# Two loads of the first block's rows move from SyncE's queue to ScalarE's

## The reference

```
scale = cond @ norm_w.T + 1.0
ms = mean(x * x, axis=-1)
h = x * (scale[:, None, :] * rsqrt(ms + EPS))
val, gate = split(h @ up_w.T)
h = val * gelu(gate)
y = act_quant(h) @ weight_quant(down_w).T + x
```

## Time and profile before

| | before |
|---|---|
| median of 3 runs | 745.76 us (745.72 to 745.92) |
| the profiled execution, its whole time | 745.96 us |
| its span, from the first to the last instruction | 744.1 us |
| TensorE busy | 734.2 us (99%) |
| VectorE busy | 564.0 us (76%) |
| ScalarE busy | 347.6 us (47%) |
| mean granted TensorE clock | 0.999 |

### The profile page before, as it was taken

How to read it: one execution, slowest core, us unless ns; L and a number is a source line. 1 busy time by engine, 2 the same in 40 slices (tenths; PEclk the granted TensorE clock), 3 DMA queues, 4 the chain that set the end, 5 groups by cost and what they waited for, 6 DMA issues and landing times.

```text
span 744.1 us, 14385 instructions
## 1 busy us (share of the span) xinstructions
PE 734.2 (99%) x5510; PEld 538.2 (72%) x5510; DVE 564.0 (76%) x1126; ACT 347.6 (47%) x677; POOL 101.7 (14%) x137
## 2 busy tenths in 40 slices
PE   7999999999999999999999999999999999999998
PEld 6544444444678887888778887788878887788864
DVE  5567778999888776888669875888758876586657
ACT  5889766433364442364334542355324443244424
POOL 1211477877230000000000000000000000000000
PEclk9999999999999999999999999999999999999999
DMA  8877583848554453443634445343543334363202
GB/s 326 304 264 237 183 281 118 282 164 250 181 172 130 143 188 117 122 145 104 201 108 142 128 131 161 114 160 100 155 150 103 101 100 130 118 179 104 96 30 85
DMA packets 44277, 117.35 MB, mean 158 GB/s; under 512 B 5424, under 2 KB 5680, under 8 KB 43056
## 3 DMA queue, kind: packets, MB, share of 16 engines
q1 hardware_dynamic: 44208, 116.42, 48.3%
HBM read 99.62 MB, written 16.78 MB: 156 GB/s over the span
## 4 chain that ended last, share of the span: by engine, by line
PE 96%; DVE 2%; DMA 1%; issue 1%; ACT 0%; SPq 0%; POOL 0%; DVEq 0%; ACTq 0%; POOLq 0%
PE ps_v L585 14%; PE ps_v L586 14%; PE ps_v L587 14%; PE ps_y L713 13%; PE ps_g L585 6%; PE ps_g L587 6%; PE ps_g L586 6%; PE ps_v L603 4%; PE ps_g L605 4%; PE ps_v L605 4%; PE ps_v L604 4%; PE ps_g L604 4%; PE ps_g L603 4%; PE ps_v L792 1%; DMA q<-in_up_t_dram 1%
## 5 line engine op out<-in xcount | busy, mean ns | idle before, releaser
L585 PE MATMUL ps_v<-x_hi,w_hi 128*128 128x256 f16 x968 | 263.9, 273 | 1.5 <-DVE ps_v L1155 0.8
L587 PE MATMUL ps_v<-x_hi,w_lo 128*128 128x256 f16 x968 | 263.9, 273 | 0.0
L586 PE MATMUL ps_v<-x_lo,w_hi 128*128 128x256 f16 x968 | 263.8, 273 | 0.0
L817 ACT COPY ps_g<-ps_v 128x256 f32<-128x256 f32 x96 | 34.3, 357 | 205.8 <-PE ps_v L587 205.8
L828 ACT ACTIVATE g<-ps_g,w_unscale 128x512 f32<-128x512 f32 x128 | 87.3, 682 | 69.6 <-PE ps_g L587 69.6
L1155 DVE TENSOR_TENSOR ps_v<-ps_v,p 128x256 f32<-128x256 f32 x96 | 41.3, 430 | 95.3 <-PE ps_v L587 95.0
L835 ACT ACTIVATE g<-h 128x512 f32<-128x512 f32 x128 | 81.3, 635 | 63.3 <-DVE h L1167 63.0
L585 PE MATMUL ps_g<-x_hi,w_hi 128*128 128x256 f16 x392 | 106.8, 273 | 0.1
L586 PE MATMUL ps_g<-x_lo,w_hi 128*128 128x256 f16 x392 | 106.8, 273 | 0.0
L587 PE MATMUL ps_g<-x_hi,w_lo 128*128 128x256 f16 x392 | 106.8, 273 | 0.0
L585 PEld LDWEIGHTS ps_v<-x_hi,w_hi 128*128 128x128 f16 x968 | 94.7, 98 | 15.8 <-DVE ps_v L1155 1.0
(11 more groups left out here) (139 smaller groups left out, 936.3 us busy)
## 6 DMA issues: line engine op xcount, KB each, us to landing
w_lo<-w_lo_dram SPq DMA_DIRECT2D x96, 448.0 KB, 3.3
q<-in_up_t_dram SPq DMA_DIRECT2D x16, 512.0 KB, 4.8
xt<-in_x_cols_dram SPq DMA_DIRECT2D x8, 1024.0 KB, 4.9
res<-in_x_rows_dram SPq DMA_DIRECT2D x26, 256.0 KB, 3.6
out_dram<-res SPq DMA_DIRECT2D x26, 256.0 KB, 2.8
xs<-in_x_rows_dram SPq DMA_DIRECT2D x22, 256.0 KB, 3.7
w_lo_dram<-w_lo SPq DMA_DIRECT2D x16, 256.0 KB, 4.4
dw<-in_down_t_dram SPq DMA_DIRECT2D x8, 512.0 KB, 6.4
```

Source lines behind the costliest of these rows:

```text
L585: pe.matmul(to, w_hi[:, wh:wh + P], hi, start=start and kt == 0, stop=False, skip_group_check=True)
L586: pe.matmul(to, w_hi[:, wh:wh + P], lo, start=False, stop=False, skip_group_check=True)
L587: last = pe.matmul(to, w_lo[:, wl:wl + P], hi, start=False, stop=(kt == 1), skip_group_check=True)
```

## The change

The two loads of `xs_first` leave SyncE's program and stand at the top of ScalarE's program, ahead of its first activation. Their sizes, sources, destinations and semaphores stay, and nothing waits before them. SyncE's program issues the first piece of weights directly behind `norm_sb`.

```
@@ SyncE
             sp.dma_start(cond_sb, cond_t).then_inc(consts_loaded, 16)
             sp.dma_start(norm_sb, norm_t).then_inc(consts_loaded, 16)
-            for half in range(2):
-                sp.dma_start(xs_first[:, half * 2 * D:(half + 1) * 2 * D],
-                             x_rows[0][:, half * 2 * D:(half + 1) * 2 * D]).then_inc(xs_first_loaded[half], 16)
             load_up(0)
             load_xt(0)
             load_up(1)
@@ ScalarE
+            for half in range(2):
+                act.dma_start(xs_first[:, half * 2 * D:(half + 1) * 2 * D],
+                              x_rows[0][:, half * 2 * D:(half + 1) * 2 * D]).then_inc(xs_first_loaded[half], 16)
             square(0, 0)
             square(0, 1)
             square(0, 2)
```

## The result

The changed kernel takes 748.22 us (median of 6 runs, 747.79 to 749.28), the kernel before 745.74 us in the runs beside it. The ratio is 1.0035 with an interval of 1.0025 to 1.0045: slower, by about 2.5 us. The profiled execution took 748.06 us with a span of 746.3 us, 2.2 us more than before. The forecast was 747.1 us, "within 0.2%", with a range of 745.6 to 748.2; the time lies 0.02 us above the range, and the change is nearly twice the forecast one. (The profiled execution of one experiment, e6, ran at a mean clock of 0.644, so only the first 13 us of its profile are used.)

A forecast was written before the change was run, and what follows sets the result against it. TensorE, busy 99% of the span, bounds the kernel, so only its first product's start matters. Weights and issues were worth 0, `norm_sb`'s delay +1.3: 745.76 + 1.3 = 747.1 us, range 745.6 to 748.2.

The forecast's parts named there:

- The condition's path: Start: `norm_sb` landing at 3.98, TensorE's product, VectorE's scale steps and fourth-quarter squares lead without a gap to `rsqrt(0)` at 8.75.
- Rival 3: Start: the weights, 0.94 us earlier, were the bound after all, giving 744.8 us; chance 0.04.
- rival 1: Start: no contention that counts, `norm_sb` lands within 0.2 us of 3.98, giving 745.6 to 745.9 us; chance 0.22.
- Rival 2: Start: ScalarE's table load precedes the issues, rows share with weights and `xt`, second half lands at 10.4; 748.3 us; chance 0.12.
- the delay of `norm_sb`: Start: `norm_sb` lands later because rows are issued ahead on another queue; bounds 0 and +2.2 us, taken as +1.3.
- From above: `norm_sb` behind the whole first half: Start: upper bound of `norm_sb`'s delay, +2.65 us less the 0.44 by which the rows start earlier, +2.2.
- both end together: Start: `norm_sb` and the first half of the rows would finish landing at the same time.
- piece-for-piece case: Start: queues alternate pieces, 4 KB of rows per 2 KB of `norm_sb`; delay +2.2 us at slow rate, +0.8 at faster.
- the end follows one for one: Whole kernel: a shift of TensorE's first product, at 15.66 us, goes through to the end undiminished.
- The case that I held likeliest: Start: rows contend with `norm_sb`, delaying the end by +0.8 to +2.2 us; chance 0.62.
- its upper third above 1.5 us: Chance of slower: about a third of the rows-against-`norm_sb` case lies above +1.5 us, counted as 0.2.

The follow-up runs named there:

- e6: Changed kernel with the rows in four transfers of 256 KB (2 KB packets) on ScalarE's queue instead of two of 512 KB; ratio 1.0066 to the kernel before.
- e1: Kernel before, all loads on SyncE's queue, with `norm_sb` issued behind the first half of the rows; ratio 1.0035.
- e7: Kernel before, all loads on SyncE's queue, with `norm_sb` issued behind both halves of the rows; ratio 1.0048.
- e11: Kernel before, one queue, with the first piece of the weights issued ahead of the rows' two halves; ratio 1.0022.
- e3: Changed kernel with only the second half of the rows on ScalarE's queue, the first behind `norm_sb` on SyncE's; ratio 1.0025 to the kernel before.
- e8: Changed kernel, but ScalarE issues the rows only after GpSimd's identity, 0.7 us behind `norm_sb`'s issue; ratio 1.0057 to the kernel before.
- e4: Changed kernel, but SyncE issues `norm_sb` first, level with the rows, and `cond_sb` behind it; ratio 1.0031 to the kernel before.
- e9: Kernel before with `norm_sb` alone moved to ScalarE's queue, rows staying on SyncE's; ratio 0.9991, repeated as e9 again 0.9994.
- e2: Changed kernel with table load and a one-column square put ahead of ScalarE's row issues, which still ran during the table load; ratio 1.0031 to the kernel before.
- e10: Kernel before with only `cond_sb` on ScalarE's queue; SyncE issues `norm_sb` first and the rows behind it; ratio 0.9996.

## Why the prediction was right and wrong

**Right: the path.** The condition's path set `rsqrt(0)`, at 11.73 in place of 8.75, as the working had it and the chain of waits of the kernel before didn't. e1 and e7 show it with one queue, and e11 shows the counterpart: with the weights early and the rows late, the start goes by the rows. The two issues by ScalarE took 0.90 us, the table load stood at 1.64, both hidden. Rival 3 falls by e11, rival 1 by the landing at 6.98. Rival 2 had 748.3 us, all but the measured 748.22, and that is chance: its mechanism, rows that land after 7.9 while `norm_sb` is unharmed, didn't occur. The second half was squared from 7.60, and `norm_sb` was what came late.

**Wrong: the size of one term, the delay of `norm_sb`: +1.3 forecast, +3.00 measured.** The failed sentence is "From above: `norm_sb` behind the whole first half", +2.2. Two mistakes are in it. I let the sharing begin at once, while in fact nothing of `norm_sb` moved until the transfer issued 0.45 us earlier was nearly through. And I counted one half as all that could be in front, when the second half was issued level with `norm_sb` (1.16) and took turns with it by packets, 4 KB for every 2. The "both end together" of the piece-for-piece case came out roughly (6.98 and 7.60), only the partner was the second half and not the first. e3 measures the term with one half alone in front: +1.97, inside my bounds. With the second half the remaining 1.03 come on top. The turns by packets bear on rival 2's mechanism too: I had the second half land at 10.4 by even bytes, and by even packets it landed at 11.9 in e8.

**Half right: the end follows one for one.** The first product came 2.87 us later, the span of the profiled execution 2.2. The timed medians are 2.5 us apart, and the runs of the changed kernel alone spread over 1.5 us, so only single executions carry what follows. The stretch from 186 to 232 us has the difference, first in the kernel before, then in the changed one (from:to, us, then busy time of PE, PEld, DVE, ACT, POOL, clock, DMA share, GB/s):

```profile
186.00:232.00 46.00, 44.59 (x344) 33.29 (x342) 41.82 (x68) 23.31 (x41) 11.41 (x12) 1.00 0.54 170
```

```profile
186.00:232.00 46.00, 45.13 (x340) 33.10 (x339) 41.03 (x66) 23.45 (x42) 13.32 (x14) 1.00 0.58 178
```

And TensorE's waits of the changed kernel after 18.6 us, against the earlier trace rows:

```profile
PE ps_v L582 <- DVE ps_g L1150: 0.6, 1, 0.6
PE ps_v L582 <- DVE ps_v L1155: 0.2, 1, 0.2
```

TensorE idles 1.41 us there before and 0.87 after: the first wait of the earlier trace rows, the one for L1155, is 0.2 us instead of 0.8. This is no slack that grows with the delay. Over the runs, span less first product is 728.2 to 728.5 us where that wait is 0.5 us or more (before, e1, e3, e4, e7, e9, e9 again, e11) and 727.6 to 727.8 where it is 0.2 (changed, e2, e8). Of the two groups the first has the latest start but one (e7), so it isn't the delay that decides; e10, with a wait of 0.2 us and its 1.29 us of issue, lies outside (729.2). What makes VectorE come to that step earlier or later wasn't tried. So the step of my working that took it as one for one holds within 0.6 us from the first product on. Between `rsqrt(0)` and the first product there is a second thing that varies, the pace of TensorE, told in the last section.

**The chances.** The case that I held likeliest was the right one; the bounds of its term were too narrow, so that its upper third above 1.5 us should have been nearly all of it.

## What to carry to other kernels

A load that is moved to another engine's queue doesn't get its time for nothing: ask which small transfer that stands first on the old queue, and starts the longest chain, now meets the moved megabyte level or behind it. Put the transfer that the longest chain waits for on the queue and in the place that is issued first, and move that one if anything. A chain of waits names one releaser for each step; lay the paths that end within a microsecond of each other side by side before pricing a gain.

## What the runs showed of the hardware

- Of two transfers on two queues, the one issued earlier went first. `norm_sb`, issued 0.45 us behind 512 KB on the other queue, moved 0.00 MB until 4 us in the changed kernel, and e3 has the same with the second half in front. The order can be turned: in e8 the rows were issued behind `norm_sb` and the first weights, and from 2 to 4.5 us ScalarE's queue moved none of them. Why the later one waits instead of taking turns at once no run shows.
- Issued about level, they take turns packet by packet, whatever the packets' size: 51 to 52 in e8, 65 to 65 in e6, with bytes of 2 to 1 and 4 to 1. The counts are less even at the start of e4, 80 to 57. The Trainium skill, page "DMA: Bandwidth & Descriptors", section "Queues, rings and completion order", has the turns by packets; the counts of e8 and e6 agree, but the first 2 us that `norm_sb` waited in the changed kernel and in e3 don't follow from it.
- The first transfers of an execution are slow and uneven. In the kernel before, the first half of the rows took 2.65 us behind `norm_sb`, and the next two transfers of 512 KB 1.27 and 1.25 us. Issued at 1.15 behind `cond_sb` alone, the first half was squared from 6.42 in e1 and from 6.11 in e7.
- ScalarE's DMA issue runs beside its table load (e2: 0.78 against 0.71 to 1.99).
- TensorE has two paces at the start, and the moment when it goes over to the faster differs from run to run. e9 and its repeat are the same kernel. Between 9.4 and 9.9 us e9 ran 7 matmuls and the repeat 12 (same columns as for e8):

```profile
9.40:9.90 0.50, 0.50 (x7) 0.50 (x6) 0.43 (x3) 0.01 (x1) 0.23 (x1) 1.00 0.94 393
```

```profile
9.40:9.90 0.50, 0.50 (x12) 0.49 (x10) 0.40 (x4) 0.07 (x1) 0.23 (x1) 1.00 0.92 385
```

  The four transposes behind that took 1.11 us in e9 and 0.65 in the repeat, and the first products are 0.41 us apart for it. They took 1.11 us in the kernel before, 1.01 in the changed one, about 0.75 in e1 and e7 and 0.65 in e2, e3 and e11. In each of these runs this is, to 0.01 us, what the first product moved less than `rsqrt(0)` did. The column of the granted clock says 1.00 at either pace, so it doesn't show the change. What sets its moment is open.
